# First attention: a finished query block split into float16 parts before it is turned, and turned by DMA instead of TensorE

## The reference

```
Q, K, V = xn @ Wq.T + bq, xn @ Wk.T + bk, xn @ Wv.T + bv      # 16 heads of width 64
w       = softmax(scale_h * Q_h @ K_h.T)                       # 2048 x 2048 for each head
attn    = concat over heads of (w_h @ V_h)                     # 2048 x 1024
y       = xn + (attn @ Wo.T + bo)                              # then a layernorm of y
```

## Time and profile before

| | us |
|---|---|
| median of 3 runs | 1926.13 (1925.07 to 1926.82) |
| the profiled execution, its own time | 1926.11 |
| its span, first to last instruction | 1924.3 |
| PE busy | 1852.8 (96%) |
| DVE busy | 1444.4 (75%) |
| ACT busy | 1547.6 (80%) |
| POOL busy | 1598.0 (83%) |

### The profile page before, as it was taken

The page is one execution under the profiler, slowest core; times in us unless marked ns, Lnnn a source line. Parts: engine busy times, 40 slices in busy tenths (PEclk is TensorE's granted clock), DMA queues, the critical chain, the costliest instruction groups (busy, mean ns, idle before and its releaser), DMA issues.

```text
span 1924.3 us, 55726 instructions
## 1 busy us (share of the span) xinstructions
PE 1852.8 (96%) x23471; PEld 1257.3 (65%) x23471; DVE 1444.4 (75%) x2647; ACT 1547.6 (80%) x1921; POOL 1598.0 (83%) x1025
## 2 busy tenths in 40 slices
PE   4999999999999999999999998779999999999998
PEld 3566666666666666666666666547777777767766
DVE  8798878878878878878878875567767767767652
ACT  4799999999999999999999999646666666666664
POOL 3899999999999999999999999358688787787752
PEclk8999999999999999999999999899999999999999
DMA  4200100100100100100100100100000000000000
GB/s 120 62 14 23 34 18 19 35 18 19 35 19 19 35 19 18 35 20 16 35 24 13 35 2 2 55 1 2 2 1 2 2 2 2 2 1 1 2 2 23
DMA packets 45034, 37.96 MB, mean 20 GB/s; under 512 B 8304, under 2 KB 44144, under 8 KB 44528
## 3 DMA queue, kind: packets, MB, share of 16 engines
q1 hardware_dynamic: 44544, 34.19, 7.0%
q10 hardware_dynamic: 240, 0.20, 0.0%
HBM read 8.15 MB, written 1.05 MB: 5 GB/s over the span
## 4 chain that ended last, share of the span: by engine, by line
PE 86%; DVE 4%; POOL 4%; issue 3%; ACT 1%; DMA 0%; SPq 0%; POOLq 0%; DVEq 0%; ACTq 0%
PE ST L1653 11%; PE ST L1654 11%; PE RING L1532 7%; PE OO L1615 6%; PE OO L1617 6%; PE OO L1614 6%; PE OO L1532 4%; POOL PBUF L705 3%; PE ST L1846 2%; PE ST L1852 2%; PE ST L1851 2%; PE ST L1853 2%; PE OO L1873 2%; PE OO L1875 2%; PE OO L1877 2%
## 5 line engine op out<-in xcount | busy, mean ns | idle before, releaser
L621 POOL TENSOR_TENSOR PAB<-PR,PAB 128x1024 f16<-128x1024 f32 x342 | 725.0, 2137 | 41.9 <-ACT PAB L808 40.5
L808 ACT ACTIVATE PAB<-ST,exp_scale 128x1024 f16<-128x1024 f32 x512 | 568.3, 1110 | 0.0
L1115 DVE TENSOR_REDUCE maxes<-RING 128x1 f32<-128x512 f32 x661 | 440.2, 685 | 122.3 <-PE RING L1532 117.9
L1614 PE MATMUL OO<-VP,PAB 128*128 128x66 f16 x4096 | 447.2, 192 | 2.9 <-POOL PAB L621 2.9
L1615 PE MATMUL OO<-VP,PAB 128*128 128x64 f16 x4096 | 447.7, 194 | 0.0
L1617 PE MATMUL OO<-VP,PAB 128*128 128x66 f16 x4096 | 445.7, 192 | 0.0
L806 ACT ACTIVATE PR<-ST,exp_scale 128x1024 f32<-128x1024 f32 x342 | 382.2, 1117 | 66.4 <-PE ST L1654 64.1
L1614 PEld LDWEIGHTS OO<-VP,PAB 128*128 128x128 f16 x4096 | 380.5, 96 | 78.5 <-issue 15.6
L1615 PEld LDWEIGHTS OO<-VP,PAB 128*128 128x128 f16 x4096 | 377.3, 97 | 60.6
L1653 PE MATMUL ST<-QL,KH 128*128 128x512 f16 x1024 | 388.6, 380 | 2.1 <-DVE QH L1127 1.0
L1654 PE MATMUL ST<-QH,KL 128*128 128x512 f16 x1024 | 388.8, 380 | 0.0
(11 more groups left out here) (319 smaller groups left out, 4029.2 us busy)
## 6 DMA issues: line engine op xcount, KB each, us to landing
KH<-HS SPq DMA_DIRECT2D x126, 64.0 KB, 2.0
QL<-HS SPq DMA_DIRECT2D x64, 64.0 KB, 2.0
QL<-LS SPq DMA_DIRECT2D x64, 64.0 KB, 2.0
QH<-HS SPq DMA_DIRECT2D x64, 64.0 KB, 2.0
KL<-LS SPq DMA_DIRECT2D x63, 64.0 KB, 2.0
X<-in_L_attn_a_x SPq DMA_DIRECT2D x4, 256.0 KB, 4.0
SHARED<-in_rope_cos SPq DMA_DIRECT2D x1, 1024.0 KB, 5.2
SHARED<-in_rope_sin SPq DMA_DIRECT2D x1, 1024.0 KB, 7.8
```

The source lines that it names most:

```text
L621: pool.tensor_tensor(PB[:, s, :], PRA[g % PR_SLOTS], PA[:, s, :], ALU.subtract).then_inc(p_low_ready, 1)
L808: act.activation(PA[:, step % SLOTS_A, :], ST[step % 2][:, :], ACT.Exp, scale=scale).then_inc(sa.exps, 1)
L1115: dve.reduce_max(maxes[:, i // BLOCKS, i % BLOCKS:i % BLOCKS + 1], bank[:, :], X_AXIS).then_inc(sa.ring_taken, 1)
L1614: pe.matmul(o, high, v[:, 0:V2_AT], start=(m == 0 and qt == 0), stop=False, skip_group_check=True)
```

## The change

For the 31 pairs that end inside the loop, the turned item is taken out of the ring. Instead DVE, right after it has normalised the second head's block at step 3 and before the two maxima of that step, splits the block in SBUF into `A2H` (a tensor_copy to float16) and `A2L` (a tensor_tensor that subtracts `A2H` from it) in the new function `split_a`. SP waits for this and issues two DMA transposes, of 128x512 float16 each, into `ATH` and `ATL`. The output item at step 7 waits for both DMAs. The 32nd pair, after the loop, is done as before. `SKIP` falls from 2 to 1 since the first unit now lacks one item, not two; the items of the ring are renumbered with that, and so the banks that they use.

```diff
+def pair_ends_a(ul, first):
+    return ((ul - 1) % UNITS_A) // BLOCKS == 1 and not (first and ul == 0)
+
+def pairs_ended_a(u):
+    return sum(pair_ends_a(v % UNITS_A, v < UNITS_A) for v in range(u + 1))
...
-    if ((ul - 1) % UNITS_A) // BLOCKS == 1 and not (first and ul == 0):
-        items += [("turned",)] if step == 3 else [("output",)] if step == 7 else []
+    if step == 7 and pair_ends_a(ul, first):
+        items += [("output",)]
...
-SKIP = 2
+SKIP = 1
...
+        A2H = sb("A2H", [P, BLK], F16)
+        A2L = sb("A2L", [P, BLK], F16)
...
             for g in range(ITER_A * G_A):                      # SP
                 head = g // STEPS_A // BLOCKS
+                u, step = divmod(g, STEPS_A)
+                if step == 3 and pair_ends_a(u % UNITS_A, u < UNITS_A):
+                    count = pairs_ended_a(u)
+                    if count > 1:
+                        sp.wait_ge(sa.ring_taken, output_item)
+                    sp.wait_ge(a2_split, count)
+                    for turned_part, part in ((ATH, A2H), (ATL, A2L)):
+                        sp.dma_start_transpose(turned_part[:, :].rearrange("p (t c) -> p t c", c=P), part[:, :]
+                                               ).then_inc(a2_turned, 16)
                 for n, item in ITEMS_A[g]:
+                    if item[0] == "output":
+                        output_item = n + 1
                     if item[0] == "project":
...
+            def split_a(qb, units_done):
+                a = A2[:, qb * BT:(qb + 1) * BT, :].rearrange("p a c -> p (a c)")
+                dve.wait_ge(a2_ready, units_done)
+                dve.tensor_copy(A2H[:, :], a).then_inc(a2_high, 1)
+                dve.wait_ge(a2_high, pairs_ended_a(units_done))
+                dve.tensor_tensor(A2L[:, :], a, A2H[:, :], ALU.subtract).then_inc(a2_split, 1)
...
                 if step == LAG_A and u:                         # DVE
                     normalise_a((u - 1) % UNITS_A, u)
+                    if pair_ends_a(u % UNITS_A, u < UNITS_A):
+                        split_a((u - 1) % BLOCKS, u)
...
-                    elif item[0] == "turned":
-                        take_turned(sa, bank, n)
...
-            def output_a(item, turned_item, pair):              # PE
+            def output_a(item, pair):
                 claim_a(item)
-                pe.wait_ge(sa.ring_taken, turned_item + 1)
                 pe.wait_ge(wo_low, 1)
...
-                elif item[0] == "turned":
-                    turned_a(n, (qb - 1) % BLOCKS, u)
-                    turned_item = n
                 else:
-                    output_a(n, turned_item, (u - 1) // UNITS_A)
+                    pe.wait_ge(a2_turned, pairs_ended_a(u) * 2 * 16)
+                    output_a(n, (u - 1) // UNITS_A)
...
             turned_a(END_A - 2, BLOCKS - 1, ITER_A * UNITS_A)
-            output_a(END_A - 1, END_A - 2, ITER_A - 1)
+            pe.wait_ge(sa.ring_taken, END_A - 1)
+            output_a(END_A - 1, ITER_A - 1)
```

More of the change, by code:

```diff
@@ L470, in build @@
         a2_ready = sem("a2_ready")
+        a2_high = sem("a2_high")
+        a2_split = sem("a2_split")
+        a2_turned = sem("a2_turned")
         xbo = sem("xbo")
@@ L1655, in scores_a @@
                 ins.then_inc(sa.scores, 1)
-            rows_item, turned_item = ROWS_LEAD, None
+            rows_item = ROWS_LEAD
             def ring_item_a(n, item, u):
-                nonlocal rows_item, turned_item
+                nonlocal rows_item
                 head, qb = divmod(u, BLOCKS)
```

## The result

The changed kernel takes 1972.47 us (median of 6 runs, 1971.93 to 1973.65). The kernel before, on the same chip, takes 1925.6 (6 runs, 1924.16 to 1926.85). The ratio is 1.0244, with a 95% interval of 1.0231 to 1.0258: slower, by 46.9 us. The prediction was 1972. The profiled execution after took 1973.65 us, 47.5 more than the profiled execution before.

What follows compares the result with a forecast made beforehand. PE was taken to set the time in the first attention's loop. Thirty pairs at 1.54 us (2.01 stall less 0.47 saved), less 0.47 for the last, gave 45.7 on 1926.1: 1972 us, range 1940 to 2055.

Steps and rivals of the forecast that it cites:

- The mechanism: In DVE's split, the copy waits for POOL's running instruction, the subtraction for the whole next one, ending at 157.31; PE stalls.
- The stall: At step 4's second maximum PE waits 2.01 us for DVE; less 0.47 saved, 1.54 us a pair, for 30 pairs.
- POOL's own loss: POOL held up by DVE's split: 0.32 + 0.55 = 0.87 us per pair, hidden in PE's stall; uncovered, 27 us.
- So I count nothing: PE's clock: stalls of 2 us in 18 could cost clock, but 16.01 busy of 20 us kept 1.00; nothing added.
- its 0.47: PE loses four float32 transposes per pair, saving 0.47 us; the last iteration's unit 7 pair was counted as keeping it.
- The DMAs: Two transposes after the split were to land between 160 and 162, or 166.5 one behind the other; taken as no wait.
- The room: From the split's end at 157.31 to PE's output at 165.4: 8.1 us for both transposes to land.
- Rival 1: Both waits and late DMAs: transposes at 5.2 us each make PE wait 2.9 more per pair; 2062 us, chance 0.13.
- Rival 2: DVE's subtraction slips in before POOL's next instruction, PE doesn't wait and the saving stands; 1911.5 us, chance 0.13.
- Rival 3: Ring slack mostly covers the wait for POOL, PE losing 0.56 us before the 0.47 saved; 1929 us, chance 0.08.

Runs made afterwards that it cites:

- split_8_columns: The changed kernel with both DVE instructions of the split cut from 512 columns to 8; 1953.18 us, ratio 1.0144.
- act_pool_split: The changed kernel with the split taken off DVE: ACT makes the copy, POOL the subtraction; 1911.74 us, ratio 0.9929.
- the seventh probe: Last of seven 128x8 two-SBUF-input DVE subtractions added to the kernel before, in the last iteration's unit 5, step 2; that kernel took 1930.62 us.
- no_split: The changed kernel without DVE's two split instructions, its DMAs transposing constant tiles and PE's waits for them kept; 1909.33 us, ratio 0.9919.
- act_high_dve_low: The changed kernel with the copy moved to ACT and the subtraction left on DVE; 1966.03 us, ratio 1.0211.
- split_alone: The kernel before with DVE's split added into tiles nobody reads, PE's transposes kept, no DMA added; 2012.84 us, ratio 1.0452.
- dve_high_pool_low: The changed kernel with the copy left on DVE and the subtraction moved to POOL; 1917.11 us, ratio 0.9953.

## Why the prediction was right

**The mechanism, right in each step of a usual pair.** The copy ends behind the end of a POOL instruction, as predicted (in unit 5 0.28 us behind it, 0.32 was worked out). The subtraction then waits for a whole POOL instruction. It ends at 157.50, when 157.31 was predicted from a unit 5 that has since moved by 0.38 us (normalising ends at 154.36, not 153.98). PE stalls at the second maximum of step 4, on DVE. split_8_columns and act_pool_split, with the ends of DVE's instructions tied to POOL's in every pair, show that the wait for POOL is the cause.

The Trainium skill (page "SBUF — State Buffer", section "Who interferes with whom") says that GpSimd and VectorE lock each other out for a whole instruction, and that the one that issues first has the ports. The first half agrees with 2.05 us for 8 columns. The second doesn't cover the 8.15 us of the seventh probe, which was issued before three POOL instructions that ran ahead of it.

**The stall: 2.01 predicted, 1.80 measured.** The term was mis-sized by 0.2 us a pair, 6 us in 30. The split lasts from the end of normalising 154.36 to 157.50, 3.14 us where 3.33 was worked out. Of those 0.19 us, 0.14 lie in POOL's middle instruction: the price of 2.13 is its recorded length, and it got through in about 1.99 (154.97 to 156.96) once it had the way. POOL's own loss was likewise smaller, 17.0 us in all (1615.0 - 1598.0) instead of 27, and it was hidden as predicted.

**The last iteration, not predicted.** Every pair was given the same stall. One got 7.22, and 2.6 us of lower clock behind it, against a term of 2.01: 7.8 us more. "So I count nothing" for the clock was right for the stalls of 2 us (1.00 in the 140 us window) and wrong for one of 7 us (0.51 after it). The row it rested on, 16 us busy out of 20, has no such long pause in one piece.

These two errors nearly cancel: -6 and +8. Two smaller ones lie beside them: the last pair doesn't save its 0.47, and the profiled loop grew by 48.7 us where 45.7 were predicted, while the rest of the program came out 1.2 shorter by itself. That 1972 stands so close to 1972.47 is luck; the working behind it is good to some 3 us, not to half of one.

**The DMAs, hidden as predicted.** The room is 157.50 to 165.59, 8.1 us. In unit 5 each issue holds SP for 1.2 to 1.3 us, twice what was assumed from the moves, and a transpose lands 2.4 or 2.5 us after its issue at the median, 4.4 at most. That leaves 4.2 us in unit 5; only the last pair waits, 0.38 us. no_split has no wait for a transpose. Rival 1 falls. The Trainium skill's 1309 ns for a 128x128 transpose (page "VectorE: DVE Perf Modes", section "The three transpose paths") does not add up block by block here: four blocks land in 2.4 us.

**The other rivals.** Rival 2 needed the split to end before 155.72; it ended at 157.50, since POOL's next instruction does get in first. Its time of 1911.5 is what the kernel takes once DVE is left out of it (1911.74). Rival 3 took the slack in the ring to cover most of the wait; a stall of 1.80 us a pair was left all the same, where rival 3 had 0.56.

## What to carry to other kernels

An instruction on DVE whose operands all lie in SBUF is not priced by its columns when POOL works without a pause on SBUF as well: price the wait for POOL's instruction, for each such instruction anew, and then look at what is queued behind it on DVE. Moving work off the bounding engine pays only if the engine that takes it can do so without that lock: here the same change cost 47 us with the split on DVE and gained 14 with it on ACT and POOL (48.7 and 10.6 in the loops of the profiled executions). Look also at the odd iterations (the first, the last), where another engine runs further ahead, before multiplying one unit's stall by the number of units.

## What was not expected of the hardware

- A DVE instruction that waits for POOL is not always served at the end of POOL's instruction. Each of the seven kernels here with such an instruction on DVE has one that waits for 3.67 to 8.57 us, in the last iteration, and is passed over up to three times. In the changed kernel POOL's next instruction had become ready 1.20 to 1.31 us before each end at which DVE was passed over, and at most 0.77 us before each at which it was served. But over all runs readiness doesn't separate the two: DVE was passed over with 0.75 (act_high_dve_low) and 0.85 us (split_alone), and served with 0.94 to 0.96 and once 1.64 (dve_high_pool_low). What decides was not shown.
- After 7.06 us without a matmul TensorE's granted clock was 0.51 from 1199 to 1205 us and 1.00 after that. The stalls of about 1.8 us a pair left it at 1.00; in split_alone, where a pair loses 2.0 to 2.7 us in several waits, it fell at three pairs (0.57 from 466 to 470 us), for about 1.7 us each.
- A DMA transpose of 128x512 float16 from SBUF to SBUF lands 2.4 to 2.5 us after its issue at the median (4.4 at most), and the issue holds SP for 1.19 us at the median for `ATH` and 1.27 for `ATL` (2.39 at most); a plain move took 0.60.
